# Local attention of a four-layer kernel: the window masks are added to the scores in PSUM by VectorE, in place of two bfloat16 mask products on TensorE

## The reference, cut to what matters

```
q, k = l2norm(q) * qs, l2norm(k) * ksc           # then rotated by position
bk2 = previous window and own window             # 64 keys for each 32 queries
mask = (it < jb) | (it > jb + w) | (jb == -1)
sim = einsum('bhwie,bhwje->bhwij', bq, bk2) * 8
sim = where(mask, -finfo.max, sim)
attn = softmax(sim, -1)
out = einsum('bhwij,bhwje->bhwie', attn, bv2)
```

## Time and profile before

| | us |
|---|---|
| time, median of 3 runs (lowest, highest) | 2366.53 (2365.16, 2367.01) |
| the profiled execution's own time | 2368.98 |
| its span | 2367.2 |
| TensorE busy | 2123.9 (90%) |
| VectorE busy | 1585.3 (67%) |
| ScalarE busy | 1753.6 (74%) |
| GpSimd busy | 1096.7 (46%) |

### The profile page before, as it was taken

One profiled execution on the slowest core, in us unless ns is written; L12 is line 12 of the kernel. 1 busy time (PEld: TensorE's weight loads), 2 busy tenths in 40 slices (PEclk: granted clock), 3 DMA queues, 4 the chain that ended last, 5 costly groups with the idle time before them and its releaser, 6 DMA issues. The chain is left out here.

```text
span 2367.2 us, 65878 instructions
## 1 busy us (share of the span) xinstructions
PE 2123.9 (90%) x26476; PEld 1010.9 (43%) x26476; DVE 1585.3 (67%) x2054; ACT 1753.6 (74%) x2574; POOL 1096.7 (46%) x461
## 2 busy tenths in 40 slices
PE   8699999999999999999999999999998687678697
PEld 3244444444444444444444444444443222223365
DVE  5566676666676676666666766767665589998432
ACT  4688878888888888888888788888886565455443
POOL 0255555455555555555555555555552025565030
PEclk8899999999999999999999999999999889999799
DMA  0332233322323223332233222333221100000011
GB/s 23 109 108 86 93 107 99 102 90 95 115 89 105 90 95 113 101 95 91 87 118 104 92 91 86 115 103 100 87 90 47 41 0 0 0 0 1 19 35 37
DMA packets 102070, 181.03 MB, mean 76 GB/s; under 512 B 15904, under 2 KB 67504, under 8 KB 101680
## 3 DMA queue, kind: packets, MB, share of 16 engines
q1 hardware_dynamic: 101776, 176.83, 23.2%
HBM read 24.73 MB, written 1.05 MB: 11 GB/s over the span
## 5 line engine op out<-in xcount | busy, mean ns | idle before, releaser
L767 POOL TENSOR_TENSOR f_shuf<-f_shuf,f_tabs 128x1024 f32<-128x1024 f32 x192 | 467.7, 2436 | 866.0 <-DMA f_shuf<-f_raw 866.0
L772 POOL TENSOR_TENSOR f_rot<-f_rot,f_shuf 128x1024 f32<-128x1024 f32 x192 | 452.8, 2358 | 15.1
L814 DVE TENSOR_REDUCE f_max<-f_ps 128x8 f32<-128x512 f32 x192 | 132.7, 691 | 302.4 <-PE f_ps L514 294.5
L670 ACT ACTIVATE f_rn<-f_ps 128x1024 f32<-128x1024 f32 x192 | 195.9, 1021 | 134.0 <-PE f_ps L492 134.0
L798 DVE TENSOR_TENSOR f_rot<-f_ps,f_tabc 128x1024 f32<-128x1024 f32 x192 | 235.1, 1225 | 51.9 <-ACT f_raw L660 49.3
L492 PE MATMUL f_ps<-f_sq,f_same 64*64 64x256 f32 x3072 | 210.1, 388 | 44.1 <-DVE f_rot L798 43.5
L806 DVE SCALAR_TENSOR_TENSOR f_qk<-f_rn,f_rot 128x1024 f32<-128x1024 f32 x192 | 233.4, 1216 | 9.5 <-POOL f_rot L772 8.0
L672 ACT ACTIVATE f_rn<-f_rn,k_lift 128x1024 f32<-128x1024 f32 x192 | 220.6, 1149 | 6.3
L480 PE MATMUL f_ps<-y_t,f_wq 128*128 128x512 f32 x384 | 217.1, 647 | 8.3 <-issue 5.5
L1200 POOL TENSOR_TENSOR s_prod<-s_state,s_cs 128x1024 f32<-128x1024 f32 x64 | 151.7, 2370 | 146.9 <-DVE s_state L1278 146.9
L824 DVE TENSOR_REDUCE f_sum<-f_ps 128x8 f32<-128x512 f32 x192 | 132.7, 691 | 119.8 <-ACT f_ps L688 119.5
(11 more groups left out here) (262 smaller groups left out, 3551.9 us busy)
## 6 DMA issues: line engine op xcount, KB each, us to landing
f_shuf<-f_raw SPq DMA_DIRECT2D x384, 256.0 KB, 2.4
f_rn<-f_rn SPq DMA_DIRECT2D x384, 128.0 KB, 2.4
e_w<-in_e_w SPq DMA_DIRECT2D x16, 256.0 KB, 2.9
f_wq<-in_f_wq SPq DMA_DIRECT2D x12, 256.0 KB, 3.4
f_wk<-in_f_wk SPq DMA_DIRECT2D x12, 256.0 KB, 4.1
f_wv<-in_f_wv SPq DMA_DIRECT2D x12, 256.0 KB, 4.0
f_wo<-in_f_wo SPq DMA_DIRECT2D x6, 512.0 KB, 4.8
f_w<-in_f_w SPq DMA_DIRECT2D x6, 341.0 KB, 4.1
```

The lines of the kernel that those rows point to most:

```text
L767: pool.tensor_tensor(view(w, 0, [S, 4], [1, S]), view(w, 0, [S, 4], [1, S]), view(tab_s, 0, [S, 2], [0, 2], [1, S]), ALU.mult).then_inc(se ...
L772: pool.tensor_tensor(t[:, :], t[:, :], w[:, :], ALU.add).then_inc(sem["rot"], 1)
```

## The change

The two mask products, their two bfloat16 tables and the copies that fill these go. The score products start their own sums (start=True). VectorE, once the scores of a pair have ended, adds the float32 mask table to banks 4 and 5 in place (an instruction of 128 partitions by 512 elements, that reads and writes PSUM and reads the mask from SBUF), and waits for its own semaphore `masked` before it takes the maximum.

```diff
@@ local_attention
-        maskb = m.mem.enter_context(nc.sbuf_tensor("f_maskb", [128, 4 * 64], mybir.dt.bfloat16))
-        identb = m.mem.enter_context(nc.sbuf_tensor("f_identb", [128, C], mybir.dt.bfloat16))
@@ semaphores
-            "w2_mm y2 fcol tab seen cross0 cross1").split()}
+            "w2_mm y2 fcol tab seen masked cross0 cross1").split()}
@@ scores
                 gather(sem["qk"], i * 8 + j + 1)
                 gather(sem["p"], i * 8 + j)
-                if isinstance(i, int) and i + j == 0:
-                    pe.wait_ge(sem["zero"], 2)
-                    pe.sem_inc(sem["seen"], 1)
                 t = qk[j % 2]
-                for h in range(2):
-                    pe.matmul(view(ps, (4 + h) * CH, [1, 256]), identb[:, :], maskb[:, :], start=True, stop=False,
-                              skip_group_check=True)
...
-                                       t[64 * h:64 * h + 64, WIN * w:WIN * w + WIN], keys, start=False, stop=True,
+                                       t[64 * h:64 * h + 64, WIN * w:WIN * w + WIN], keys, start=True, stop=True,
                                        skip_group_check=True)
@@ soft_a
                 need(dve, sem["s_mm"], i * 8 + j + 1)
+                dve.tensor_tensor(view(ps, 4 * CH, [CH, 2], [1, S]), view(ps, 4 * CH, [CH, 2], [1, S]),
+                                  view(mask, 0, [0, 2], [1, S]), ALU.add).then_inc(sem["masked"], 1)
+                need(dve, sem["masked"], i * 8 + j + 1)
                 dve.tensor_reduce(view(mx, 0, [4, 2], [1, 4]), view(ps, 4 * CH, [CH, 2], [64, 4], [1, 64]), AX.X,
                                   ALU.max).then_inc(sem["max"], 1)
@@ ahead of the first slot
-            dve.tensor_copy(maskb[:, :], mask[:, :])
-            dve.tensor_copy(identb[:, :], ident[:, :]).then_inc(sem["zero"], 1)
```

## The result

| | before | after |
|---|---|---|
| median of 14 runs each, on the same chips (lowest, highest), us | 2368.12 (2365.16, 2374.68) | 2381.69 (2374.02, 2387.34) |
| ratio | | 1.0058, 95% interval 1.0046 to 1.0069 |
| profiled execution's own time, us | 2368.98 | 2380.20 |
| its span, us | 2367.2 | 2378.4 |

The kernel becomes slower by 0.58%, some 13.6 us. The forecast had 2373.8 us and a range of 2359 to 2384: the sign is right, the time lies in the range, and the 7.3 us that were forecast are about half of what came.

A forecast was written before the change was run, and what follows sets the result against it. TensorE was taken to bound some slots, VectorE's chain others. Regular units -2.8, first unit +1.9, special units +4.6, +2.1 and +1.5 sum to +7.3 us on 2366.5: 2373.8 us, range 2359 to 2384.

The forecast's parts named there:

- first unit: Unit without extras: six slots go from 7.33 to 7.75 us, slots 0 and 6 save 0.31 each; +1.9 us.
- slots 3 and 4 of units 3, 7, 11, 15, 19: Tiny VectorE copy waits for GpSimd's later product, the next addition follows: extra 0.91 us each, +4.6 beyond the regular sum.
- slots 3 and 4 of units 5, 9, 13, 17, 21: Slot 3 already waits for line 833, slot 4 lacks a hiding delay: estimated +0.3 us each, +1.5 beyond the regular sum.
- slot 0 behind the loop's jump: Units 5, 9, 13, 17: VectorE starts late, line 833 decides slot 0, +0.31 us instead of -0.22; +2.1 extra.
- What TensorE gets back: Dropping two mask products saves 0.22 us per slot where TensorE sets the pace, 0.31 where scores wait for line 833.
- Rival A: TensorE gets the mask products' whole 0.38 us per slot back, not 0.22: -11.1 us, 2355 us; chance 0.15.
- What the addition takes: VectorE's addition over 128x512 in PSUM takes 0.69 us, 0.72 from its start to the maximum's.
- Rival C: The addition in PSUM takes some 0.80 us: +9.2 us, 2383 us; chance 0.10 together with Rival D.
- The regular slots: Slots 0 to 2 -0.66 together, then +0.36, -0.14, +0.09, -0.09, +0.32: -0.12 us per unit, -2.8 over 23 units.
- over 60 such waits: Sign: score products (line 514) wait for line 833 in slot 3 of every unit, over 60 waits instead of 35.
- rival B: Special units don't pay, weight DMAs and the jump set their slots: -0.9 us in all, 2365.6 us; chance 0.20.
- Rival D: The copy (line 877) falls behind GpSimd's start in regular units too: +25 us; chance 0.10 together with Rival C.

The follow-up runs named there:

- e11: The kernel before once more, unchanged, for a second trace; a single run, 2366.57 us.
- e1: The changed kernel without VectorE's addition, so no mask at all; 2342.76 us, ratio 0.9897 to the kernel before.
- e2: The kernel before, mask products kept, plus a VectorE addition of zeros over the same PSUM; 2413.04 us, ratio 1.0186.
- e6: The kernel before without the softmax's maximum and subtraction, mask products kept; 2362.65 us, ratio 0.9977.
- e8: The changed kernel with the nine-column copy (line 872) moved from VectorE to ScalarE; 2367.48 us, ratio 0.9999 to the kernel before.
- e12: The changed kernel with the nine-column copy still on VectorE in slot 3, but between `straight` and `normalise`; 2371.97 us, ratio 1.0005 to the kernel before.
- e3: The changed kernel with the nine-column copy written as a tensor_tensor maximum instead of tensor_scalar; 2382.56 us, ratio 1.0067 to the kernel before.
- e10: The kernel before with the nine-column copy moved from VectorE to ScalarE; 2361.15 us, ratio 0.9977.

## Why the prediction was right, and where it was not

By its own steps, from the traces of before and after (the columns are sums over the 24 units):

| term, us | forecast | measured |
|---|---|---|
| first unit | +1.9 | +2.5 |
| slots 3 and 4 of units 3, 7, 11, 15, 19 | +5.7 | +1.1 |
| slots 3 and 4 of units 5, 9, 13, 17, 21 | +2.6 | +6.9 |
| slots 3 and 4 of unit 20 | +0.2 | +2.8 |
| slot 0 behind the loop's jump, slot 7 ahead of it | +2.5 | +3.4 |
| all other slots of 23 units | -5.6 | -5.6 |
| the slots together | +7.3 | +11.1 |

(The forecast's -0.12 a unit is spread here over the rows it belongs to. In the first unit slots 2 to 5 and 7 grew by 0.41 each and slot 6 lost 0.31, as forecast. The other 0.6 us are slot 0: the forecast had it bound by `raw` and 0.31 shorter, but at full clock it takes 7.33 before, in e11, and 7.75 after. A stretch at a lower clock, in slot 0 before and in slot 1 after, costs 1.4 and 1.3 us and nearly cancels.)

- **What TensorE gets back: right.** 0.22 per slot, shown by e1 and after (25.74) against before and e2 (26.39). Rival A, with 0.28 or more, fell. Line 506 keeps the 0.07 ahead of the modelled end of what comes before (839.32 against 839.39). The Trainium skill (TensorEngine Tiling (Array Packing), Key Properties) says that a change of tiling mode drains the array; this trace agrees, with line 506 starting 0.59 after the transposes. At the 0.49 of the earlier trace rows, where the mask pair followed the transposes, the saving would have been 0.31, and it is 0.22.
- **What the addition takes: right.** 0.70 with 0.73 to the maximum, forecast 0.69 and 0.72. Rival C (0.80) fell, though its time, 2383, came close: another mechanism with the same price. The estimate of 0.66 from the Trainium skill (VectorE: DVE Perf Modes, TRN2 errata table) was too low by 0.04.
- **The regular slots: right to 0.05.** -0.65, +0.40, -0.14, +0.09, -0.14 and +0.29 against -0.66, +0.36, -0.14, +0.09, -0.09 and +0.32. Slot 3 ends at 7.79 and not at 7.75. The addition starts at 0.93 of the slot and not at 0.90, since VectorE is busy with line 868 until then, and it and the maximum behind it are each 0.01 longer; so the exponential comes 0.71 later and not 0.67. One of the signs failed in its form: "over 60 such waits" of the scores for line 833 were not counted, there were 34. In slot 3 line 490 waits for `straight` first, and the transposes then end so close to line 828 that nothing is left to be called idle; the growth stands at line 490, 51 waits to 123.
- **Who set slots 4 to 6: half right.** "TensorE sets the pace in some slots and VectorE in the others" holds for the waits, but with 1.4 us less work on VectorE (e6) slots 4 and 5 of unit 10 keep their 7.89 and 10.18, and slot 6 has 9.69 in place of 9.74. ScalarE sets them: it is busy 7.79, 10.08 and 9.62 us there. The slot-by-slot working took its queue into account, and so came out right.
- **The special units: the step that was mis-sized.** "Units 5, 9, 13, 17, 21 ... +0.3 each, +1.5, an estimate between 0 and 0.6" measured 6.9 in place of 2.6, beyond its bound, unit 20 wasn't counted, and "units 3, 7, 11, 15, 19 ... extra 0.91 each" measured 1.1 in place of 5.7. The mechanism was named for the wrong units.
- **Units 5, 9, 13, 17, 21.** In units 5, 9, 13 and 17 the copy starts at 8.29, 8.41, 8.66 and 8.06 of slot 3 where it started at 7.34, 7.31, 7.58 and 7.45: 0.6 to 1.1 later, as the chain from the slot before, over GpSimd's late products, carries the addition of that slot too (the first product of slot 3 starts 0.97, 1.10, 1.09 and 0.62 later). GpSimd's next product moves less (unit 9 from 7.49 to 7.76). So the copy falls behind its start and lasts 1.7 to 2.0 us; in units 17 and 21 it did so before the change too, in 21 no longer. But the copy isn't all of it. Of the 6.9 us, 4.4 lie in the slots 4 of the five units, which e8 and e12 bring back to 7.75 each. The other 2.5 lie in the slots 3, 39.7 us before and 42.2 after, and are still there with the copy on ScalarE (42.5 in e8): `normalise` waits there for GpSimd's late product, 0.40 to 1.00 us in units 5, 9, 13 and 17 after and 0.53 to 1.18 in e8.
- **Units 3, 7, 11, 15, 19.** Here the copy was already behind the start of GpSimd's product, and the first product of slot 3 starts at 1.24, 1.56, 1.67, 1.53 and 0.95, against 1.42, 1.38, 1.08, 1.52 and 1.69: no common shift, as rival B had it, whose half of the argument held. Where such a unit keeps a long copy (3, 11, 15) its two slots grow by 0.64, 1.59 and 0.77, with 1.13 forecast; where it loses it (7, 19) they shrink by 0.51 and 1.42. Which of them has a long copy changes from run to run.
- **That the copy's place costs most of it is shown**, not only read: moved off VectorE (e8) or ahead in its slot (e12) it gives back 14.0 and 12.5 us by the ratios; in another form at the same place (e3) nothing. Of 13.7 us, 8.5 go with the copy, and 5.2 remain with it out of the way in both kernels; the intervals leave some 3 us on that. In the traces of e8 and e10 slots 3 and 4 of units 5, 9, 13, 17 and 21 (+4.3), those of unit 20 (+1.5), slot 0 behind the jump (+3.1) and the first unit (+1.5) take what the other slots gain. Unit 20 keeps a longer slot 3 in both, 8.99 and 9.18: there `normalise` waits for a DMA (`f_rn`), whose second transfer lands 4.41 us after its issue where 2.4 is usual; why was not settled. Only its slot 4 was the copy's. Slot 3 of unit 20 after:

```profile
1573.56 1.23 DVE L798 SCALAR_TENSOR_TENSOR f_qk<-f_rn,f_rot 128x1024 f32<-128x1024 f32 x1 [1.30 <-DMA f_rn<-f_rn]
```

- **Rival D**, a long copy in regular units, fell: these have it at 7.56 of the slot and GpSimd from 7.64 on, 6.85 and 6.94 before. In the nearest of them the order holds by under 0.1 us, in both kernels. The mechanism was the right one, in the units whose products come late by a DMA. The "five or seven units, not more" with a long copy were eight; before has seven.
- **The last 4 us.** Of the 7.9 us between 2373.8 and 2381.7, 3.9 lie in the slots. Another 1.6 is the reference, whose median over 14 runs is 2368.1, not 2366.5; and 2.4 is that the two profiled executions stand differently to their medians (0.9 above before, 1.5 below after).

## What to carry to other kernels

Read a trade between two engines slot by slot, and put the same care into the few units that don't repeat: the regular ones here came out within 0.1 us, nearly all of the surprise sat in 11 of 24. A tiny instruction on VectorE whose operands are all in SBUF is a hazard when GpSimd may start first: list each with its distance to GpSimd's next start, and place it where the engine waits for GpSimd anyway. Where GpSimd's product waits for a transfer, a delay added to the chain can shift such an instruction by more than the product: a margin of some 0.15 us was lost that way in units 5 and 9, while in the regular units, where both moved together, 0.08 was kept.

## What the runs showed of the hardware

- A VectorE instruction of 0.16 us over 128x9 lasts 1.72 to 2.35 us behind `soft_c`, when it starts behind a GpSimd product in SBUF, and 0.46 to 0.88 us in e12, when it starts near the product's end; in all these places it ends within 0.04 us of it. It is the same as `tensor_scalar` (one input in SBUF) and as `tensor_tensor` (two), and a `scalar_tensor_tensor` over 128x1024 goes from 1.22 to 3.25. On ScalarE the same copy takes 0.20 to 0.22 in three traces. The Trainium skill (SBUF — State Buffer, Who interferes with whom) says that the two engines share a pair of ports which the first to start holds for its whole instruction; every row here agrees. It also lists both forms of the copy, so by that section the result of e3 was to be expected. VectorE's instructions with an input in PSUM keep their time behind a product (the maximum, 0.69, in 168 places after). The other order shows too. A product of GpSimd that starts while `normalise` runs on VectorE ends later: line 767 in unit 3 before starts at 336.76, `normalise` runs from 336.19 to 337.42, and the product takes 2.88 instead of 2.36. Over 2.45 us are 35 of GpSimd's products before and 3 after, which is most of what GpSimd's busy time loses by the change:

```profile
L767 POOL TENSOR_TENSOR f_shuf<-f_shuf,f_tabs 128x1024 f32<-128x1024 f32 x192 | 467.7, 2436 | 866.0 <-DMA f_shuf<-f_raw 866.0
L759 POOL TENSOR_TENSOR f_shuf<-f_shuf,f_tabs 128x1024 f32<-128x1024 f32 x192 | 453.9, 2364 | 888.7 <-DMA f_shuf<-f_raw 888.7
```

- Behind the loop's jump VectorE sits idle ahead of its first instruction, 1.76 to 1.89 us before and 1.58 to 2.54 after, and slot 0 grows by 0.54 to 1.54 in units 5, 9, 13 and 17, where 0.31 was forecast. The first addition of unit 5 in the trace after:

```profile
452.47 0.70 DVE L806 TENSOR_TENSOR f_ps<-f_ps,f_mask 128x512 f32<-128x512 f32 x1 [2.44 <-issue]
```

  It starts 3.19 after its scores (449.28), against the 2.15 of before; in units 9, 13 and 17 it is 2.55, 3.54 and 2.95 against 1.97, 2.16 and 2.08. Of this 0.50 to 0.86 is VectorE's last instruction ahead of the jump (line 883, once 888), which ends that much later in slot 0. The rest is the idle time, and that isn't shown to be the addition's: kernels without one reach 2.33 (e1) and 2.52 (e10). In e1 these slots are 0.17 shorter than before, on average.
- The granted clock differs from run to run in a few places. After, slot 1 of the first unit had a mean clock of 0.67 and took 9.08 where its neighbours take 7.75, and slot 5 of unit 3 had 0.85 and took 10.89 instead of 10.27:

```profile
104.59:113.67 9.08, 8.14 (x92) 3.45 (x93) 5.93 (x8) 5.38 (x7) 4.71 (x3) 0.67 0.27 87
346.35:357.24 10.89, 10.08 (x131) 4.92 (x131) 6.62 (x9) 10.36 (x17) 7.11 (x4) 0.85 0.24 77
```

  Part of each was at the lower level (1.2 GHz), the rest at 2.4. In the slot ahead of the first TensorE was busy 4.96 of 7.75 us, in the slot ahead of the second, behind the long copy, 7.33 of 9.28. The kernel before has one such slot too, slot 0 of the first unit, 8.73 in one trace and 7.33 in the other, so no rule for this change is drawn from it.
